# Setup folds inside the second slot's program, values projected to token rows, state-space maps as narrow array tiles

## What is computed

```python
x = x + _L0_xattn_ref(ctx, _layernorm(x), ...)   # 16 heads of 64 over context and latents
x = x + _L0_attn_ref(_layernorm(x), ...)         # gated linear recurrence ("rnn")
x = x + _L0_ffn_ref(_layernorm(x), ...)          # low-rank experts ("lora")
x = x + _L1_xattn_ref(_layernorm(x), ctx, ...)
x = x + _L1_attn_ref(_layernorm(x), ...)
x = x + _L1_ffn_ref(_layernorm(x), ...)
x = x + _L2_xattn_ref(ctx, _layernorm(x), ...)   # 8 heads of 64 over context and latents
x = x + _L2_attn_ref(_layernorm(x), ...)
x = x + _L2_ffn_ref(_layernorm(x), ...)
x = x + _L3_xattn_ref(_layernorm(x), ctx, ...)   # x3: x@W1.T + mean(ctx)@W2.T + b
x = x + _L3_attn_ref(_layernorm(x), ...)         # state space ("ssm")
x = x + _L3_ffn_ref(_layernorm(x), ...)

# in _L0_xattn_ref and _L2_xattn_ref:
q = ln @ Wq;  k, v = split(kv_input @ Wkv)
attn = softmax(q k^T);  return (attn @ v) @ Wout + bout
# in _L3_attn_ref, for each token:
h = h * 0.9 + 0.1 * (xt @ w_B);  y = (h @ w_C) * silu(z)     # 256 -> 16 states -> 256
```

## Time and profile before

| | us |
|---|---|
| median of three runs | 2697.71 (2694.99 to 2702.02) |
| the profiled execution, its own time | 2693.03 |
| its span, first to last instruction | 2691.2 |
| PE busy | 2442.0 (91%) |
| DVE busy | 1499.1 (56%) |
| ACT busy | 1197.8 (45%) |
| POOL busy | 844.0 (31%) |
| mean granted clock of TensorE | 0.978 |

### The profile page before, as it was taken

How to read it: one execution, slowest core, us unless ns; L and a number is a source line. 1 busy time by engine, 2 the same in 40 slices (tenths; PEclk the granted TensorE clock), 3 DMA queues, 4 the chain that set the end, 5 groups by cost and what they waited for, 6 DMA issues and landing times.

```text
span 2691.2 us, 39615 instructions
## 1 busy us (share of the span) xinstructions
PE 2442.0 (91%) x15456; PEld 1512.2 (56%) x15456; DVE 1499.1 (56%) x3904; ACT 1197.8 (45%) x2948; POOL 844.0 (31%) x788
## 2 busy tenths in 40 slices
PE   6989988998999998998999999988999999999989
PEld 4555554555556565564655555555565555555555
DVE  3556565554455566656544656655455465665453
ACT  3544343445454444444644453434454445354533
POOL 2334242322223334332322433422322143434300
PEclk7999999999999999999999999999999999999998
DMA  5000000000000000000000000000000000000000
GB/s 208 1 1 1 1 9 1 9 8 9 9 1 9 1 1 9 1 9 8 9 9 1 9 1 2 8 1 16 1 5 8 5 1 1 1 1 1 1 1 8
DMA packets 6090, 25.92 MB, mean 10 GB/s; under 512 B 784, under 2 KB 784, under 8 KB 5136
## 3 DMA queue, kind: packets, MB, share of 16 engines
q1 hardware_dynamic: 5904, 23.40, 2.4%
HBM read 21.30 MB, written 2.10 MB: 9 GB/s over the span
## 4 chain that ended last, share of the span: by engine, by line
PE 65%; DVE 21%; ACT 6%; POOL 4%; issue 3%; DMA 0%; DVEq 0%; POOLq 0%; SPq 0%
PE ps L445 8%; PE ps L462 6%; PE ps L525 6%; PE ps L484 6%; PE ps L549 3%; PE ps L790 3%; PE ps L517 3%; PE ps L413 3%; PE ps L468 2%; POOL small L1686 2%; PE ps L512 2%; PE ps L515 2%; DVE small L1240 2%; PE ps L571 2%; DVE P L1253 2%
## 5 line engine op out<-in xcount | busy, mean ns | idle before, releaser
L1702 POOL TENSOR_TENSOR P<-P,small 128x384 f32<-128x384 f32 x384 | 317.3, 848 | 613.6 <-DVE small L1275 613.5
L1010 ACT ACTIVATE P<-ps,small 128x192 f32<-128x192 f32 x768 | 313.3, 420 | 215.0 <-DVE small L1267 214.5
L1686 POOL TENSOR_TENSOR small<-small,mhalf 128x4 f32<-128x4 f32 x112 | 151.5, 1353 | 705.7 <-DVE small L1258 555.4
L462 PE MATMUL ps<-kvT,big 128*128 128x192 f32 x1536 | 307.8, 338 | 20.7 <-ACT P L1010 9.9
L1267 DVE TENSOR_REDUCE small<-ps 128x2 f32<-128x384 f32 x384 | 210.3, 552 | 130.7 <-PE ps L462 123.1
L462 PEld LDWEIGHTS ps<-kvT,big 128*128 128x128 f32 x1536 | 244.3, 190 | 68.7 <-ACT P L1010 43.1
L445 PEld LDWEIGHTS ps<-wts,P 128*128 128x128 f32 x1920 | 234.0, 192 | 57.1 <-issue 41.8
L445 PE MATMUL ps<-wts,P 128*128 128x128 f32 x1920 | 256.9, 281 | 4.0 <-DVE X L1327 2.1
L1766 POOL TENSOR_TENSOR P<-T 128x512 f32<-128x512 f32 x96 | 124.3, 1296 | 222.2 <-ACT T L1151 116.5
L468 PE MATMUL ps<-cst,P 128*128 128x128 f32 x1152 | 164.7, 278 | 28.3 <-POOL P L1702 13.5
L484 PE MATMUL ps<-kvT,score 128*128 128x512 f32 x384 | 175.7, 600 | 3.7 <-ACT T L988 2.8
(11 more groups left out here) (278 smaller groups left out, 4550.8 us busy)
## 6 DMA issues: line engine op xcount, KB each, us to landing
ctok<-ctok_dram SPq DMA_DIRECT2D x8, 512.0 KB, 3.5
ctxT<-ctx_dram SPq DMA_DIRECT2D x8, 512.0 KB, 3.6
wts<-weights_dram SPq DMA_DIRECT2D x1, 3208.0 KB, 28.0
big<-fold_dram SPq DMA_DIRECT2D x3, 1024.0 KB, 7.0
wts<-weights_dram SPq DMA_DIRECT2D x1, 2304.0 KB, 21.0
X<-x_dram SPq DMA_DIRECT2D x8, 256.0 KB, 6.3
out_dram<-X SPq DMA_DIRECT2D x8, 256.0 KB, 2.0
wts<-weights_dram SPq DMA_DIRECT2D x1, 1029.0 KB, 15.2
```

What stands on the lines that cost most here:

```text
L462: m = pe.matmul(ps[s][:, at:at + KEYS], big[s][:, BANK * b + 128 * p:BANK * b + 128 * p + 128], kvT[s][:, keys_at(b):keys_at(b) + KEYS], s ...
L1010: m = act.activation(probs(s, b // 2)[:, to:to + KEYS], ps[s][:, at:at + KEYS], ACT.Exp, bias=small[s][:, 4 * e + p:4 * e + p + 1], accum_ ...
L1686: pool.tensor_tensor(rstd(s, name, n), variance(s, name, n), mhalf[:, 0:n], ALU.pow).then_inc(*sig("rstd", s))
L1702: m = pool.tensor_tensor(view, view, over(small[s][:, at:at + 2], 2, [128, 2, KEYS]), ALU.mult)
```

## The change

1. **Setup.** The loads are in another order: the first slot's residual, the q and k folds' sources, columns, constants, the first slot's context, the v and output sources (now in `big[1]`), the second slot's residual and context, the sources of the second attention's folds. Ahead of `weave` PE makes only the q·k products of the first attention and the q bias; the v·Wout products, both products of the second attention and the output bias are the first steps of the second slot's program (`fold_rest`, on PE, ACT and DVE). The first slot normalises its latents first, and its context is turned behind the first projection of the latents (`context_first`). The bf16 constants are cast in DVE's `fold_rest`. The output bias is now a row of 128 features, made by 8 matmuls of 128x128.
2. **Values to token rows.** The mixed probabilities are stored by tile of 128 tokens and head (`mixed_at`); `out_of(t)` makes tile t of the output with 8 matmuls whose stationary operand is 128 tokens of one head and whose moving operand is 128 columns of `value`. Tiles 0, 1 and 2 stand between the steps of the fourth pair, tile 3 at the end. DVE adds the bank straight to the residual, for each g; the copies to `tmp(s, 3)` and the turns are gone. The bias is added to the residual by POOL (`preset_heads`) in the middle of g = 0. The projection of g = 1 uses the banks in the other order, so that its first step doesn't wait for the sum of g = 0.
3. **Narrow tiles.** w_B is applied with 32 output columns at four places (partitions 0 and 64 for the first half of the channels, 32 and 96 for the second), without accumulation; w_C is applied with 64 rows for each output half. In x3 the four matmuls of W1 come first and the eight of the mean behind them.
4. **Order.** All strings of `ORDER` are new.

```diff
 # SP, ahead of weave
+                load(0)
                 sp.dma_start(big[0][:, 0:2048], fold[:, 0:2048]).then_inc(w_fold_qk, 16)
-                sp.dma_start(big[0][:, 2048:4096], fold[:, 2048:4096]).then_inc(w_fold, 16)
-                sp.dma_start(big[1][:, 0:2048], fold[:, 4096:6144]).then_inc(w_fold, 16)
                 sp.dma_start(col[:, :], cols[:, :]).then_inc(w_col, 16)
                 sp.dma_start(cst[:, :], consts[:, :]).then_inc(w_cst, 16)
+                load_context(0)
+                sp.dma_start(big[1][:, 0:2048], fold[:, 2048:4096]).then_inc(w_fold_vo, 16)
+                load(1)
+                load_context(1)
+                sp.dma_start(big[1][:, 2048:4096], fold[:, 4096:6144]).then_inc(w_fold2, 16)
...
 # PE, heads
+        def qp_bank(g, r):
+            return 2 * ((r + (g == 1)) % 2)
+                    def out_of(t):
+                        if t == 0 and i == 0:
+                            pe.wait_ge(fold_act, 7 if g == 2 else 5)
+                        for k in range(8):
+                            at = 128 * block_of(h0 + k, nh)
+                            m = pe.matmul(part(s, 1, t), big[s][:, 1024 * t + 128 * k:1024 * t + 128 * k + 128], value[:, at:at + 128],
+                                          start=(t == 0 and k == 0), stop=(t == TILES - 1 and k == 7))
+                        return m
...
-                        elif r == 0:
-                            pe.wait_ge(*on("h0_sb", s, i))
+                        elif r == 1 and g == 1:
+                            pe.wait_ge(*on("h0_x", s, i))
                         elif r == 1 and g == 0:
+                            if context_first:
+                                yield from context_first
+                                yield
                             pe.wait_ge(*on("zT", s, i, "ctx.kv"))
...
                         turn_p(j, 2, 0)
                         if j < PAIRS - 1:
                             yield from scores(2 * j + 2)
+                        else:
+                            yield
+                            pe.wait_ge(*on("exped", s, i, 2 * (u + 1) + 1))
+                            out_of(0)
                         yield
                         pe.wait_ge(*on("p_ready", s, i, u + 1))
                         turn_p(j, 3, CTX)
+                        if j == PAIRS - 1:
+                            yield
+                            out_of(1)
                         yield
                         pe.wait_ge(*on("pT_act", s, i, 2 * v))
                         turn_p(j, 2, PAIR - CTX)
                         if j < PAIRS - 1:
                             yield from scores(2 * j + 3)
+                        else:
+                            yield
+                            out_of(2)
...
-                    for r in range(4):
-                        yield
-                        if r == 0:
-                            pe.wait_ge(*on("mix_act", s, i, 4 * g + 3))
-                            pe.wait_ge(*on("mix_dve", s, i, 4 * g + 3))
-                        for k in (2 * r, 2 * r + 1):
-                            m = pe.matmul(bank(s, 1), value[:, 128 * block_of(h0 + k, nh):128 * block_of(h0 + k, nh) + 128],
-                                          by_head(s, k), start=(k == 0), stop=(k == 7))
-                    m.then_inc(*sig("heads_ps", s))
-                    if g:
-                        yield
-                        pe.wait_ge(*on(f"h{g}_sb", s, i))
-                        for t in range(TILES):
-                            m = pe.transpose(part(s, 0, t), tile_of(tmp(s, 3), t), C("ident"))
-                        m.then_inc(*sig("y_ps", s))
+                    yield
+                    pe.wait_ge(*on("mix_act", s, i, 4 * g + 3))
+                    pe.wait_ge(*on("mix_dve", s, i, 4 * g + 3))
+                    out_of(3).then_inc(*sig("heads_ps", s))
...
 # PE, x3 and ssm
                         pe.matmul(part(s, 1, t), tile_of(Z[s], t), W("x3a"), start=(t == 0), stop=False)
+                    for t in range(TILES):
                         for bb in range(2):
...
-                        m = pe.matmul(bank(s, 0), tile_of(W("ssm_B"), k), P[s][:, 1024 + GT * k:1024 + GT * k + GT],
-                                      start=(k == 0), stop=(k == 1))
+                        for p0 in (32 * k, 64 + 32 * k):
+                            m = pe.matmul(bank(s, 0, 1, p0, p0 + 32), W("ssm_B")[:, 32 * k:32 * k + 32],
+                                          P[s][:, 1024 + GT * k:1024 + GT * k + GT], start=True, stop=True)
...
-                        m = pe.matmul(bank(s, k), tile_of(W("ssm_C"), k), tmp(s, 1), start=True, stop=True)
+                        m = pe.matmul(bank(s, k), W("ssm_C")[64 * k:64 * k + 64, :], tmp(s, 1)[64 * k:64 * k + 64, :], start=True, stop=True)
...
 # PE, slot 1 runs this ahead of its first pass
+                def fold_rest():
+                    yield
+                    pe.wait_ge(w_fold_vo, 16)
+                    pe.wait_ge(fold_act, 4)
+                    for h in range(H0):
+                        j, hh, at = h // 2, h % 2, 128 * block_of(h, H0)
+                        m = pe.matmul(ps[1][:, at:at + 128], rows(1, "v0T", j, hh), rows(1, "o0", j, hh), start=True, stop=True)
+                    m.then_inc(folded, 1)
+                    yield
+                    pe.wait_ge(w_fold2, 16)
+                    pe.wait_ge(fold_act, 5)
...
+                    yield
+                    pe.wait_ge(fold_act, 6)
+                    for j in range(H0 // 2):
+                        at = FOLD_AT["o0"][0] - 2048 + 128 * j
+                        m = pe.matmul(ps[1][:, 0:128], V("bv0", j).to_broadcast([128, 128]), big[1][:, at:at + 128],
+                                      start=(j == 0), stop=(j == 7))
+                    m.then_inc(folded, 1)
+                    yield
+                    pe.wait_ge(fold_act, 7)
+                    pe.wait_ge(fold_dve, 1)
...
 # DVE, heads
-                    if g == 1:
-                        yield
-                        dve.wait_ge(*on("heads_ps", s, i, g))
-                        dve.tensor_tensor(tmp(s, 3), bank(s, 1), tmp(s, 3), ALU.add).then_inc(*sig("h1_sb", s))
-                    if g:
-                        yield from add(s, i, f"h{g}", 0)
+                    if g == 0:
+                        yield
+                        dve.wait_ge(*on("x_biased", s, i, "h0"))
+                    yield
+                    dve.wait_ge(*on("heads_ps", s, i, g))
+                    if g == 1:
+                        dve.wait_ge(*on("h0_x", s, i))
+                    m = dve.tensor_tensor(res(s, i), bank(s, 1), res(s, i), ALU.add)
+                    if g:
+                        link(m)
+                    else:
+                        m.then_inc(*sig("h0_x", s))
 # POOL
+                def preset_heads(s, i):
+                    yield
+                    if i == 0:
+                        pool.wait_ge(fold_dve, 1)
+                    pool.wait_ge(*on("tok", s, i - 1, "x0"))
+                    pool.tensor_tensor(by_tile(res(s, i)), by_tile(res(s, i)), over(obias0[:, :], 1, [128, TILES, D]), ALU.add)\
+                        .then_inc(*sig("x_biased", s))
```

249 lines of the change are left out of this document (136 added, 113 removed).

## The result

The changed kernel takes 2620.3 us (median of 4 runs, 2618.32 to 2628.49), the kernel before 2697.41 in the same session: ratio 0.9718, 95% interval 0.9694 to 0.9742. That is 77 us or 2.8% faster. The prediction said 2661, 2636 to 2684: the direction was right, the gain was more than twice the forecast one, and the time lies under the range.

The account below looks back on a forecast made before the run. PE's work, busy for 91% of the span, was taken as the bound, its idle time second. Terms of -18 + 8 - 11 - 3 + 3 - 8 - 5 = -34 from 2693.03, plus half of a 4.7 us offset, gave 2661; range 2636 to 2684.

Parts of the forecast that it names:

- Setup, -18: Start of the kernel: first scores 15 us earlier and 3 us of early idle time filled; bounds -10 to -22.
- The work of values: Value projection on PE: small matmuls +11, splits +4, dropped turns of L532 -7; +8 us in all.
- rival 5: Value projection: small matmuls 2.5 times as dear for each column, 240 us more, 2900; chance 0.01.
- The fill, -11: Fourth pair of the heads: value tiles 0 to 2 fill half of PE's 21.9 us idle; ends 0 and -22.
- links in the chain of each slot: End of heads: a copy or add and the turn leave the way to the residual add; -3 us, 0 to -15.
- x3 -8, w_C -5: Layers: grouping x3's matmuls saves 1.0 us and 64-row w_C 0.66 us, 8 times each; -8 and -5 us.
- w_B 0: State-space map: four 32-column matmuls run side by side in pairs, taking the same time as two full ones; 0 us.
- The order's 12 us either way: New order strings, not priced from the profile: 12 us added to the range on both sides.
- Of the rivals, 1: Only the start is won; fourth-pair idle time moves to the group's end, at L413; 2675 us, chance 0.25.
- Rival 2: Idle ahead of L512 and L468 goes whole, a quarter of L413's wait too, setup 22; 2634 us, chance 0.12.
- Rival 3: Moved folds and new order stall PE for both slots, a fifth more body idle time; 2713 us, chance 0.05.
- Rival 4: Narrow tiles don't overlap: w_B costs +14 and w_C brings nothing; 2680 us, chance 0.06.

Follow-up runs that it names:

- values_only: Changed kernel with all folds ahead of both slots and x3, w_B and w_C as before, keeping the changed order; 2660.93 us.
- setup_ahead: Changed kernel with all folds ahead of both slots and the loads in their old order, order strings kept; 2641.30 us.
- the two refits of before: Kernel before with only its order strings fitted anew by a search, twice with different random seeds; 2641.16 and 2643.52 us.
- values_refit: values_only with its order strings fitted anew, starting from its own order; 2613.70 us.
- setup_refit: setup_ahead with its order strings fitted anew, starting from its own order; 2594.37 us.
- after_refit: Changed kernel with only its order strings fitted anew by the search; 2575.85 us.
- link_1: Changed kernel with one more DVE copy between the last value tile and the add to the residual; 2644.10 us.
- link_4: Changed kernel with four more DVE copies between the last value tile and the add to the residual; 2718.07 us.
- values_late: Changed kernel with value tiles 0 to 2 moved behind the fourth pair, right ahead of tile 3, other order steps kept; 2748.03 us.
- late_refit: values_late with its order strings fitted anew by the search; 2653.22 us.
- narrow_only: Kernel before with the narrow tiles and regrouped x3 alone, old order strings unchanged; 2686.57 us.

## Why the prediction was wrong

The parts in the changed order, taken off one after the other (values_only, setup_ahead, the changed kernel), and with fitted orders (the mean of the two refits of before, values_refit, setup_refit, after_refit). In the kept order the differences are uncertain by 5, 11 and 12 us, in the fitted ones by some 7 each:

| part | forecast | kept order | fitted orders |
|---|---|---|---|
| values (+8 - 11 - 3 + 3) | -3 | -35 | -28 |
| narrow tiles (-8 - 5) | -13 | -19 | -20 |
| setup | -18 | -23 | -16 |
| sum | -34 | -76 | -65 |

Since values_only and setup_ahead start 3 us later than the kernel before (54.02 and 54.41 against 50.97), the row of the setup holds some 3 us in the kept order that belong to the row of values.

- **Setup, -18: right**, though the start was won by 12.3 and not 15 us: the waits for copies and the half-speed projection took 3 us more than I gave them. "First scores before 42 us" held.
- **The work of values: right for the matmuls.** 7.1 to 7.3 us for each block against 7.34 forecast, and nothing for the splits, which had +4; L532's turns gone. The small matmuls were not dear, rival 5 is out: 1.79 us for 8 is 0.22 us each. What the sum lacked is that the turns of the probabilities take 6 to 7 us less.
- **The fill, -11: right in kind, somewhat less in size.** Idle time ahead of the mix and behind POOL, the two rows of L512 and L468, is down by 7.2 us from 21.9; within the fourth pairs, from first turn to mix, all idle time is down by 5 (13.2 to 8.0).
- **"Gone with it are links in the chain of each slot ... PE works for the other slot meanwhile; I count -3, from 0 to -15": this step failed.** The mechanism was named, but the term was too small by some 25 to 30 us, because its price was wrong. From the last value matmul to the end of the add to the residual the way got 37 us shorter in 16 places (50 to 13), and with what follows, up to the normalised residual, 42 (120 to 78). "PE works for the other slot meanwhile" was the reason for a small number. link_1 and link_4 lengthen just this way, at 24 places, and pay 1.3 to 1.4 us for each microsecond: PE takes both slots' steps in a fixed order, so lateness on this way stands in front of the other slot's work as well. At that price 37 us would be some 50; the kernel before had an order fitted to its longer way, and values_only with everything else in it gained 35. The wait behind this way is also where the idle time went: 18 of 19 us after the first scores.
- **It was not the value block that left the way.** Behind the mix only a quarter of it remains, and from the fourth mix to the last value matmul the sum of 24 places fell from 312 to 204 us. But the three other pieces stand in the fourth pair of the same slot: from that pair's first turn the sum is 390 us before and 456 now. What their place brings is work for PE where it would wait. values_late shows that the changed order depends on this place (125 us), and late_refit, with its start from a misfit, doesn't say what it is worth in an order of its own.
- **x3 -8, w_C -5: right as work** (8.3 and 5.3). **w_B 0: mis-sized**, since the two pairs also run beside each other where they stand together: some 3 us less. I had also set it against the length of a row, 1.98; from start to start those two full matmuls take 1.82 (2603.09 to 2604.91). With the half speed in these layers the three fell by 17 us in narrow_only, which brought 12 of time, and by 20 in the changed kernel, which brought 19 to 25. The Trainium skill, "TensorEngine Tiling (Array Packing)", section "Key Properties", says that a change of the tiling mode drains the engine; x3 without its alternation fell from 3.05 to 2.11, which agrees.
- **Presets on POOL, +3**: they took 1.27 us each, not 1.10; no run separates what they cost.
- **The clock was not in the sum at all.** The kernel before runs 92.6 us at half speed, the changed one 58.0. At 0.45 this is 16 of the 44 us of busy time. It multiplies whatever changes the idle time, up or down.
- **The order's 12 us either way were far too few in a misfit (170, 192) and about right for how well each given order fits its own code (56 and 43 to gain, 13 apart).**

Of the rivals, 1 fell: the idle time didn't move to the group's end, it fell there most. Rival 2 ("more than forecast") had the mechanism, with a quarter of L413's wait to go; it lost 17 of 59 us after the start, yet the time came out 14 us below even this rival's. Rival 3 is refuted for this order and shown for a foreign one. Rival 4 is out: the narrow tiles overlap. What would have shown in the profile: "PE's busy time 5 to 10 below" was wrong, "idle time after the start below 228" right (209: 220.5 less 11.2 before the first scores).

What stays open is how the 28 to 35 us of values part into the fill, the shorter way and the clock in an order fitted to each. No run takes only the copy and the turn out of the kernel before, or splits the value block and keeps them.

## What to carry to other kernels

A copy and a turn that only hand a result on cost the bounding engine little, yet the next step of their stream waits for them; read their length from the trace, with the time for which the turn stands in the queue. Where engines take two streams in one fixed order, any microsecond added to a stream's way shifts both; price it at one to one and a half, not at what the share of the chain suggests. Whether a block that was split and moved left the way is seen only over the whole stretch into which its pieces went: here the end got 108 us shorter in sum and the whole 66 longer. Fit the order again after the change (here 43 to 56 us in either kernel, 1.6 to 2.1%), and never judge a code by an order carried over from another: the same instructions were 170 us apart.

## What the runs showed of the hardware

An idle gap of PE costs more than itself: with 51 us more idle time in link_4 came 99 us more at a granted half speed, and 44 us more busy time for the same matmuls. The clock's column can't be trusted at the very start: it reads 1.00 over the first 38.71 us of the changed kernel, while two matmuls of L518 take 3.54 us to their successor there (17.42 to 20.96) and 1.8 later (83.17 to 84.99). Two matmuls of 32 output columns at partitions 64 apart take 0.98 us together, where one full-width one took 0.86; four of them, two for each half of the channels, took 1.00 us (717.90 to 718.90, and twice in setup_ahead), where two full-width ones take 1.82. In other layers the four took 1.46 to 1.6 at the full clock; the runs don't say what decides. A POOL add over the same 128x512 took 1.27 us in `preset_heads` against 1.10 in the earlier trace rows; the runs don't say why.
